# One launch, twelve stages: an expert stage with a ring of sixteen middle tiles, softmax sums made by TensorE, an earlier share copy, and a router's ranking over four quarters

## The reference, cut to what matters

```python
# L0_attn, L1_attn: causal softmax attention, 16 heads
attn = softmax(where(causal, q @ k.T * scale, -max)); y = attn @ v
# L0_ffn: 8 experts of 128 -> 512 -> 128, all of them run on all tokens
probs = softmax(x @ Wr + br); gate = probs * (cumulative probability before it in falling order, top one always)
h = relu(x @ W1[e] + b1[e]);  y = sum_e gate[:, e] * (h @ W2[e] + b2[e])
# L2_xattn (with clip), L3_xattn: 16 heads of 8 features, 77 keys
attn = clip(q @ k.T * scale, -10000, 10000)            # L2 only
attn = softmax(attn); attn = where(any(isnan(attn)), 1 / 77, attn)   # the where in L2 only
out = (attn @ v) @ Wo + bo
# L2_ffn: 16 experts; expert e takes the 64 tokens with the largest logits[:, e]
logits = xn @ router_weight.T + router_bias
_, idx = top_k(logits.T, 64)        # of equal logits the earlier token
```

## Time and profile before

| | us |
|---|---|
| median of 3 runs (lowest to highest) | 1623.77 (1612.93 to 1628.18) |
| the profiled execution, as timed | 1619.06 |
| its span, first to last instruction | 1617.3 |
| PE busy in the span | 1460.7 (90%) |
| DVE / ACT / POOL busy | 999.3 / 675.9 / 394.6 |
| mean granted TensorE clock | 0.949 |

### The profile page before, as it was taken

One profiled execution on the slowest core, in us unless ns is written; L12 is line 12 of the kernel. 1 busy time (PEld: TensorE's weight loads), 2 busy tenths in 40 slices (PEclk: granted clock), 3 DMA queues, 4 the chain that ended last, 5 costly groups with the idle time before them and its releaser, 6 DMA issues. The chain is left out here.

```text
span 1617.3 us, 25581 instructions
## 1 busy us (share of the span) xinstructions
PE 1460.7 (90%) x9683; PEld 911.0 (56%) x9683; DVE 999.3 (62%) x1912; ACT 675.9 (42%) x1656; POOL 394.6 (24%) x403
## 2 busy tenths in 40 slices
PE   7999999999999898998788984885999999999996
PEld 5666565544665556556577853662444566664434
DVE  4676373443455655645649437759887886567864
ACT  3775352233356644442420223542455666660002
POOL 3000031000100010003620304427777553510001
PEclk7999899999879999999989997997999999999998
DMA  2000000510000000000030300111110101179990
GB/s 91 2 2 1 3 1 8 204 39 26 15 1 1 2 1 16 9 10 3 1 122 7 118 10 30 48 31 23 40 39 27 26 16 21 27 176 247 255 239 14
DMA packets 24053, 78.98 MB, mean 49 GB/s; under 512 B 4936, under 2 KB 6774, under 8 KB 23552
## 3 DMA queue, kind: packets, MB, share of 16 engines
q1 hardware_dynamic: 23072, 74.26, 16.8%
q10 hardware_dynamic: 864, 3.15, 0.7%
HBM read 72.11 MB, written 1.08 MB: 45 GB/s over the span
## 5 line engine op out<-in xcount | busy, mean ns | idle before, releaser
L193 PE MATMUL psum<-ident 128*128 128x128 f32 x1360 | 181.4, 291 | 55.6 <-DVE wide L2108 20.9
L193 PEld LDWEIGHTS psum<-ident 128*128 128x128 f32 x1360 | 169.9, 204 | 74.6 <-DVE wide L2108 21.5
L510 DVE TENSOR_REDUCE quad_max<-psum 128x1 f32<-128x128 f32 (+3 forms) x256 | 113.5, 485 | 97.5 <-PE psum L403 97.3
L184 POOL TENSOR_TENSOR rstd<-var,minus_half 128x4 f32<-128x4 f32 x30 | 30.6, 1021 | 579.6 <-DVE var L143 545.1
L472 ACT ACTIVATE pt<-psum,quad_max 128x128 f32<-128x128 f32 (+3 forms) x256 | 133.3, 524 | 84.7 <-DVE quad_max L510 80.9
L2557 PE MATMUL psum<-slots,xn_t 128*128 128x512 f32 x256 | 113.2, 602 | 19.6 <-DVE pt L2707 19.6
L2578 PE MATMUL psum<-pt,slots 128*128 128x512 f32 x256 | 113.8, 598 | 3.3 <-DVE pt L2719 2.2
L2323 ACT ACTIVATE p<-psum,duo_max 128x512 f32<-128x512 f32 x128 | 86.7, 682 | 64.7 <-DVE duo_max L2358 62.5
L2358 DVE TENSOR_REDUCE duo_max<-psum 128x1 f32<-128x512 f32 x128 | 82.3, 684 | 35.6 <-PE psum L2245 35.4
L419 PE MATMUL psum<-ident,pt 128*128 128x128 f32 x640 | 91.7, 288 | 8.4 <-DVE p L527 7.3
L2557 PEld LDWEIGHTS psum<-slots,xn_t 128*128 128x128 f32 x256 | 49.5, 194 | 82.6 <-issue 57.0
(11 more groups left out here) (474 smaller groups left out, 2944.8 us busy)
## 6 DMA issues: line engine op xcount, KB each, us to landing
pt<-scratch_out_gates SPq DMA_DIRECT2D x32, 256.0 KB, 11.5
heads<-scratch_out_gates SPq DMA_DIRECT2D x24, 256.0 KB, 14.1
slots<-in_s_l0f SPq DMA_DIRECT2D x8, 514.0 KB, 3.6
wide<-scratch_gates SPq DMA_DIRECT2D x8, 512.0 KB, 7.0
slots<-in_s_l3v SPq DMA_DIRECT2D x8, 512.0 KB, 3.6
context_v<-scratch_out_gates SPq DMA_DIRECT2D x16, 256.0 KB, 18.3
slots<-in_s_l3o ACTq DMA_DIRECT2D x6, 512.0 KB, 10.2
weights<-in_w_l1a SPq DMA_DIRECT2D x1, 2624.0 KB, 9.4
```

Of the source, the lines that this page charges most:

```text
L193: nc.tensor.matmul(m.ps[bank][:, 0:P], m.ident[:, :], m.ident[:, :], start=True, stop=True, skip_group_check=True)
L510: nc.vector.tensor_reduce(m.quad_max[:, n % 2, g:g + 1], m.ps[g][:, 0:keys], AX.X, ALU.max, negate=True).then_inc(m.quad_negmax, 1)
```

## The change

Four pieces, made together.

1. *Quad attention.* DVE's share copy moves ahead of the maxima of heads 2 and 3; ACT's `take_ahead` moves from the end of the iteration to between its second and third exponential.
2. *First layer's experts.* 16 middle tiles (`hidden_all`, in `pt`) in place of four; the second matmul follows 14 pieces behind the first; the turn of the gates stands ahead of piece 10 and the biases ahead of piece 14 of the first pass, which is unrolled on PE; the 32 `keep_busy` matmuls there go. The pairs of the gate chain move to `p`.
3. *Crosses with few keys.* The exponentials are turned and multiplied as they are; 16 more matmuls, with columns of ones (`cols4`), give the sums in the same bank; DVE divides 128 x 128 at the end of every second step. DVE's sum and reciprocal, POOL's product, the two `keep_busy` matmuls of a step and ACT's last copy go. In l2x the test for NaN is made of the sums so found.
4. *Router by quarters.* logits as 4 x 32 partitions x 256 tokens; eight rounds on those, then eight on the 4 x 64 found, for the limit; masks by token; counting of the tokens before each by bf16 matmuls with a triangular matrix and a matrix of ones. POOL makes these two matrices at the start of its part of the stage. `keep_busy` 115 becomes 48 + 3 + 5 + 6.

To stay within the semaphores, the first eight of `rows_in` (last stage) are those of `expert_in` with an offset.

```diff
 # quad_scalar
                 if g == 1 and a.ends_group(i - 3):
                     take_output((i - 3) // a.group_sets)
+                if g == 1 and a.projects(i - 1):
+                    take_ahead((i + 2) // NQ)
...
-        if a.projects(i - 1):
-            take_ahead((i + 2) // NQ)
 # quad_vector
+        if a.ends_group(i - 3):
+            group = (i - 3) // a.group_sets
+            wait(dve, m.quad_scaled, m.inverted0[a.name] + group - 1)
+            bank = turn_filled(dve, m, a.share[group])
+            nc.vector.tensor_copy(m.quad_times[:, group % 2, :], bank).then_inc(m.quad_taken[a.share[group][0]], 1)
         if i < SETS:
             maxima(i, (2, 3))
...
 # l0_ffn_tensor
+HIDDEN_LAG, GATES_BEHIND = 14, 10
-    keep_busy(nc, m, 32)
-    pe.wait_ge(m.gates_ready, 1)
...
+        for k in range(16 + HIDDEN_LAG):
+            if isinstance(i, int) and k == GATES_BEHIND:
+                turn_gates()
+            if isinstance(i, int) and k == HIDDEN_LAG:
+                begin_output()
...
-            q = k - 2
+            q = k - HIDDEN_LAG
...
-    with pe.Fori(0, E0 // 2) as i:
+    one_pass(0)
+    with pe.Fori(1, E0 // 2) as i:
         one_pass(i)
 # l0_ffn_scalar
+            if isinstance(i, int) and k == GATES_BEHIND:
+                for j in range(2):
+                    bank = read(m, act, f"l0fg{j}")
+                    nc.scalar.activation(m.gate_t[0:E0, j * S:(j + 1) * S], bank[0:E0, :],
+                                         ACT.Copy).then_inc(emptied(m, f"l0fg{j}"), 1)
             act.wait_ge(m.hidden_ready, h0 + 16 * i + k + 1)
-            wait(act, m.hidden_used, h0 + 16 * i + k - 3)
+            wait(act, m.hidden_used, h0 + 16 * i + k - 15)
 # narrow_cross, tensor
-                pe.wait_ge(m.probs_ready, a.s0 + n + 1)
+                pe.wait_ge(m.exp_done, a.s0 + n + 1)
                 wait(pe, m.cross_taken, a.x0 + n)
-                keep_busy(nc, m, 2, 4)
...
+                for j in range(GROUP):
+                    for g in range(GROUP):
+                        last = nc.tensor.matmul(bank[own(g), P:2 * P], m.cols4[0:SC, j, 0:32],
+                                                m.xpt[0:SC, g // 2, g % 2 * GROUP + j, qt * P:(qt + 1) * P], start=False,
+                                                stop=j == GROUP - 1, skip_group_check=True)
+                last.then_inc(filled(m, name), 1)
 # narrow_vector (new; the maxima as in cross_vector), n = k - 6
+        if n >= 0 and n % 2 == 1:
+            u = n // 2
+            at = slice(u * P, (u + 1) * P)
+            bank = read(m, dve, f"{stage}o{u}")
+            d.done(nc.vector.reciprocal(m.k_t[:, at], bank[:, P:2 * P]))
+            nc.vector.tensor_tensor(m.o_t[:, at], bank[:, 0:P], m.k_t[:, at], ALU.mult).then_inc(emptied(m, f"{stage}o{u}"), 1)
+            if a.clip:
+                d.done(nc.vector.tensor_reduce(m.numbers[:, u:u + 1], m.k_t[:, at], AX.X, ALU.add))
 # l2_ffn_tensor
+    for c in range(4):
+        last = nc.tensor.matmul(bank[32 * c:32 * c + 32, 0:QUARTER], w["router"], m.xn_t[:, c * QUARTER:(c + 1) * QUARTER],
+                                start=True, stop=True)
...
+    keep_busy(nc, m, 48)
+    pe.wait_ge(m.router_limit, 1)
...
+    keep_busy(nc, m, 3)
+    pe.wait_ge(m.masks_ready, 1)
+    count_to(nc, m, bank, m.level_bf)
+    for t in range(NT):
+        last = nc.tensor.matmul(bank[:, P:P + E2], m.ones_sq[:, :], m.above_bf[:, t, :], start=False, stop=t == NT - 1,
+                                skip_group_check=True)
...
+    keep_busy(nc, m, 5)
+    pe.wait_ge(m.masks_ready, 2)
+    count_to(nc, m, bank, m.above_bf).then_inc(filled(m, "l2fd0"), 1)
+    keep_busy(nc, m, 6)
 # count_to (new)
+    last = nc.tensor.matmul(bank[:, 0:P], m.up_to[:, :], mask[:, :, :].rearrange("p t e -> p (t e)"), start=True, stop=False,
+                            skip_group_check=True)
+    for t in range(NT - 1):
+        rest = NT - 1 - t
+        last = nc.tensor.matmul(bank[:, (t + 1) * E2:P].rearrange("p (n e) -> p n e", e=E2), m.ones_sq[:, :],
+                                mask[:, t:t + 1, :].broadcast_to([P, rest, E2]), start=False, stop=t == NT - 2,
+                                skip_group_check=True)
 # l2_ffn_vector
+    largest(m.logits[:, 0:QUARTER], m.left[:, 0:QUARTER], m.lists[:, 0, :])
+    for c in range(4):
+        last = nc.vector.tensor_copy(m.places[0:E2, c * CAP:(c + 1) * CAP], m.lists[32 * c:32 * c + E2, 0, :])
+    d.done(last)
+    largest(m.places[0:E2, 0:QUARTER], m.left[0:E2, 0:QUARTER], m.lists[0:E2, 1, :])
+    nc.vector.tensor_copy(m.limit_wide[0:E2, :], m.lists[0:E2, 1, CAP - 1:CAP].broadcast_to([E2, P])).then_inc(m.router_limit, 1)
...
```

More of the change, by code:

```diff
@@ L990, in l0_ffn_tensor, with turn_gates, begin_output @@
     last.then_inc(filled(m, "l0fr"), 1)
-    keep_busy(nc, m, 32)
-    pe.wait_ge(m.gates_ready, 1)
[L993 to L1004, removed]
+    def turn_gates():
+        pe.wait_ge(m.gates_ready, 1)
+        for j in range(2):
+            bank = fill(m, pe, f"l0fg{j}")
+            for t in range(4):
+                last = nc.tensor.transpose(bank[0:E0, t * P:(t + 1) * P], m.gates[:, 4 * j + t, :], m.ident[:, :])
+            last.then_inc(filled(m, f"l0fg{j}"), 1)
+    def begin_output():
+        for j in range(2):
+            copied(m, pe, f"l0fg{j}")
+        for j in range(2):
+            bank = fill(m, pe, f"l0fy{j}")
+            nc.tensor.matmul(bank[:, :], w["b2"][0:E0, :], m.gate_t[0:E0, j * S:(j + 1) * S], start=True, stop=False,
+                             skip_group_check=True)
     g0, h0 = m.slot0["l0f"], m.h0["l0f"]
@@ L1733, in vector @@
             copied(m, dve, f"{stage}h0")
-            for b in range(B):
-                copied(m, dve, f"{stage}o{b}")
+            for n in range(B * NQ - 2, B * NQ):
+                copied(m, dve, f"{stage}o{n}")
             for b in range(B):
@@ L1766 @@
 CAP = T // E2
+QUARTER = T // 4
 EXPERT_LAG, EXPERT_SLOTS = 3, 8
@@ L1901, in l2_ffn_vector @@
     m.turns_dve += 2
-    for j in range(2):
-        copied(m, dve, f"l2fr{j}")
-    src = m.logits[0:E2, :]
-    for r in range(CAP // 8):
-        d.done(nc.vector.max(m.top8[0:E2, r % 2, :], src))
-        if r < CAP // 8 - 1:
-            d.done(nc.vector.match_replace(m.left[0:E2, :], m.top8[0:E2, r % 2, :], src, -BIG))
-            src = m.left[0:E2, :]
-    limit = m.top8[0:E2, (CAP // 8 - 1) % 2, 7:8]
-    above, level, count = m.left[0:E2, :], m.places[0:E2, :], m.running[0:E2, :]
-    one = m.ones_col[0:E2, 0:1].broadcast_to([E2, T])
@@ L1930, in l2_ffn_vector, with largest @@
[L1930 to L1937 removed]
+    def largest(src, left, lists):
+        for r in range(CAP // 8):
+            top = lists[:, 8 * r:8 * r + 8]
+            d.done(nc.vector.max(top, src))
+            if r < CAP // 8 - 1:
+                d.done(nc.vector.match_replace(left, top, src, -BIG))
+                src = left
@@ new lines, in l2_ffn_vector @@
+    nc.vector.engine_nop().then_inc(m.masks_ready, 1)
+    d.done(nc.vector.tensor_reduce(m.per_token[:, 1, :], logits, AX.X, ALU.max))
+    d.done(nc.vector.tensor_tensor(probs, logits, last16(m.per_token[:, 1, :]), ALU.subtract))
+    nc.vector.engine_nop().then_inc(m.router_less_max, 2)
+    bank = read(m, dve, "l2fc0")
+    d.done(nc.vector.tensor_scalar(m.needed[:, :], bank[:, P:P + E2], -1.0, float(CAP), ALU.mult, ALU.add))
+    nc.vector.tensor_tensor(m.place[:, :, :], by_tile(bank[:, 0:P]), each(m.needed[:, :]), ALU.is_le).then_inc(
+        emptied(m, "l2fc0"), 1)
```

185 lines of the change are left out of this document (107 added, 78 removed).

## The result

The changed kernel took 1578.86 us (median of 4 executions, 1572.03 to 1607.61), the kernel before beside it 1625.97 (median of 4): a ratio of 0.9707, 95% interval 0.9618 to 0.9796. The prediction was 1579.0. The profiled execution took 1573.58 us, with a span of 1571.8 and a mean clock of 0.955. One of the four executions, at 1607.61, is left out of the interval; the experiments point to the changed kernel itself as its cause, and not to a disturbance from outside.

What follows compares the result with a forecast made beforehand. It saw TensorE near its bound in l1a and l3x, a three-engine chain pacing l2x, and serial DVE chains in l0f and the router. Terms -7.3 - 5 + 0 - 14 - 13.5 = -39.8 from 1619.1 gave 1579 us, range 1563 to 1597.

Steps and rivals of the forecast that it cites:

- Sum: Whole kernel: the gains of all stages added, -39.8 us from the profiled execution's 1619.1 us.
- Quad, -7.3: Quad attention, l1a: moving the share copy into DVE's idle time removes six stalls of TensorE's transposes, -7.3 us.
- the bound of -10: Quad attention: the largest gain allowed, -10 us, if ACT's earlier take also shortens ACT's chain.
- Experts, -5: First layer's experts, l0f: earlier first piece, second pass 3.3 to 5.0 us sooner, other passes 0.3 us shorter each; -5 us.
- l2x, -14: Layer 2's cross: 15 steps fall from 56.7 to about 43 us, start some 3 us sooner, end some 3 longer; -14 us.
- TensorE is the bound: l2x's steady steps: POOL, DVE and ACT all need under 2.97 us a step, so TensorE sets the pace.
- l3x, 0: Layer 3's cross: steady steps unchanged, mean 2.97 against 3.0 us, start sooner, end longer; 0 us, bounds -4 and +4.
- Router, -13.5: Router in l2f: shorter matmul and copy 1.1, finding the limit 3.9, work behind the limit 8.5; -13.5 us.
- A: Rival, whole kernel: gains overlap with what is late next, such as another wait or late reloads; 1601 us, chance 0.10.
- D: Rival, crosses: the sum matmuls don't run four abreast, 2.4 us more for each of 16 sets; about 1618 us, chance 0.03.
- C: Rival, whole kernel: more gain than the sum, with fewer half-clock stretches; 1564 us, chance 0.17.
- B: Rival, crosses: without the identity matmuls TensorE falls to 1.2 GHz, 15 steps take 81 us; 1653 us, chance 0.03.

Runs made afterwards that it cites:

- e1: Changed kernel with DVE's share copy back behind the maxima and ACT's `take_ahead` back at the iteration's end; l1a took 186.0 us.
- e2: Changed kernel with only ACT's `take_ahead` back at the iteration's end, share copy still early; l1a took 179.04 us, l2x 103.2 us.
- e10: The changed kernel run again without any edit; six executions from 1571.1 to 1607.3 us, l2x 80.6 us in its profile.
- e4: Changed kernel with the first two expert slots loaded ahead of layer 1's weights and the gates awaited after 9 tiles; l0f took 127.5 us against 135.2.
- e5: Changed kernel without the 16 sum matmuls of every second step in both crosses; l3x took 64.9 us, 6.0 less.
- e7: Changed kernel with 66 in place of 48 identity matmuls before the router's limit; 1604.1 us, its router stage 1.3 us shorter.
- e11: Changed kernel without the 20 identity matmuls in steps 1 and 2 of l2x; executions 1606.7 to 1610.5 us, l2x 103.0 us.
- e12: e11's kernel with two identity matmuls added in each of l2x's later twelve steps; 1585.26 us, l2x 84.5 us.

## Why the prediction was right, and where it was not

- **Sum.** -39.8 predicted, -45.5 in the profiled execution. The median hit 1579.0 because two of the other three executions lay higher than the profiled one (1573.58), and one of them had the long fall of the clock that the sum left out. That is luck of 5 us within a range of 34.
- **Quad, -7.3.** Right by its own reason: e1 gives 7.3 us of waits back. But l1a differs by 8.6 at an equal clock, 1.43 us a group where the wait was 1.21. It lies within the bound of -10, though not by the bound's reason: without ACT's earlier take (e2) the groups are as short. Where the other 1.3 us come from is open. How much the clock moves this stage shows in e10: the 20.5 us stretch did not come, and l1a took 170.9.
- **Experts, -5.** -3.7, and each step is in the profile: a first piece at 292.7 in the old time (292.2 predicted), a first product that ends 0.4 us late, a wait for it of 2.28 us (2.5). The second pass came at 329.05, where 326.8 to 328.5 stood, the later end for a fall of the clock in that wait. It fell there, for 3.4 us, and the 0.4 us by which the product was late came on top: this is the term that was mis-sized, -2.8 us for -3.3 to -5.0. The landing of 10.4 us was taken as given; e4 shows that it hangs on the order of two loads.
- **l2x, -14.** The 15 steps took 41.5 us (about 43), 15.2 less than before; the start was 3.5 us sooner (3), the end longer by 3.4 (some 3). One size was off: the reciprocal of 128 x 128 costs 0.96 us, not 0.3; only the last one is on the path. And "TensorE is the bound" is half right: by the row with 0.48 us of waiting the short step is the loop of transposes and take. In l3x, by e5, 6.0 of the sums' 8.1 us are on the path.
- **l3x, 0.** -0.6: the start 0.5 us sooner, the 15 steps 2.3 shorter, the end 2.1 longer. Steps of 2.27 and 3.63 us (2.2 and 3.7).
- **Router, -13.5.** -15.9: 1.5 for the matmul and its copy (1.1), 12.1 from the first maximum to the first selection (12.4), and 2.3 that I had not counted: the selections' matmuls took 13.97 us where they had 15.55, with less of them at half clock, and the stretch from the stage's start to the router matmul was 0.7 shorter, which the change does not touch (8.2 us; 8.9 before and in e7).
- **Rivals.** A did not happen: no gain was eaten by the wait next in line. D neither, 1.0 us for a set of sums. C was the nearest of them to the profiled execution (1564 against 1573.6), but the forecast was nearer, and of C's gains only the router's came in full (-15.9 for -15).
- **B, the clock, with 3 in 100,** is where the reasoning was wrong although the number was right. It said that both crosses would fall, and argued against it with the steady steps, in which TensorE is busy for 5.4 of 6.0 us. The place was wrong: in the steps of l3x the clock fell in no profile, and in l2x it is the first steps that count, of which the prediction counted only that they get shorter. The price was too high: 15 steps at half clock took 68.5 us (e11), where it had 81, as a pair took 10.1 and not 10.8 and the first steps carry no values. The chance was too low: by the times it happened in 3 of 10 executions. Such an execution lies at 1600 to 1608, outside the range, still faster than before. The Trainium skill (TensorE: Matmul & The Clock Gate, Part 1) says that throttled is the default and activity releases it. e12 agrees, as with two more matmuls a step the clock came back; e11 does not show it, as there the records have TensorE busy for 58.7 of 60 us and the clock stayed at half.

## What to carry to other kernels

Before identity matmuls are taken out of a pipelined loop, look at its first turns and not only at its steady state: there they fill waits that the finished pipeline does not have, and what they guard against costs 29 us here against some 1 us of filling. Take them out of the steady steps, where they are on the path (7 to 8 us a stage), and leave them in front of the waits of the start, each as long as the idle time in that row. And time such a kernel many times: one profile in which it kept its clock says little about the next.

## What the runs showed of the hardware

- TensorE at half clock and busy for 58.8 of 60 us stayed there to the end of the stage (81.9 and 92.2 us, e2 and e11); with 4 more identity matmul records in a step it was back after 20.5 us (e12), and without them after 6.8 us in e1 and e4 and 17.1 in e10. That the records show TensorE busy is thus no sign that the clock will return.
- DVE's reciprocal of 128 x 128 float32 took 0.96 us, a product of the same size 0.29, both read from PSUM.
- MAX8 took 0.43 us over 128 x 256 and 1.22 over 16 x 1024; over 16 x 256 it took 0.42. So here it costs by the elements in a partition, and 128 partitions take as long as 16.
- Two loads change places in what they delay when their order of issue is changed: the first slot (514 KB) landed 10.9 us after issue behind layer 1's weights (2,624 KB), and in e4, ahead of them, TensorE did not wait for it 7.6 us after issue.
